# Four graph layers on one core: the second layer's tiles turned by DMA, four banks for its projections, weight low parts moved on VectorE, feature rows padded

## The chip, the core and the metric

The kernel runs on one core of one Trainium2 chip. The metric is the time of one execution on the device in microseconds (us), the lower the better. The engines are TensorE (PE), VectorE (DVE), ScalarE (ACT), GpSimd (POOL) and SyncE (SP); the last issues most DMAs.

## The reference

x is 2048 × 256, adj a sparse 2048 × 2048 matrix of zeros and ones. Four layers follow each other, each `x = layernorm(x + layer(x))`:

```
L0(x) = adj @ (x W0) + b0                                     # W0: 8 heads side by side, 256 x 256
L1(x) = mean over 4 heads of softmax(leaky_relu(src_i + dst_j, 0.01) + adj_ij) @ (x W)
                                                              # src, dst = (x W) . a, two vectors a head
L2(x) = relu(conv(h, W2, b2) + h), h = conv(x, W1, b1)        # conv(f) = relu([f, adj @ f] W + b)
L3(x) = relu(D^-1/2 (adj + I) D^-1/2 x W3)                    # D: row sums of adj + I
```

## The kernel before

Rows are cut into T = 16 tiles of 128. Every factor that goes into a matmul is split into a high and a low float16 part (hi = f16(v), lo = v - hi); a product is hi·hi + hi·lo + lo·hi. adj stays in SBUF as bf16 for the whole kernel; SP loads it in 16 blocks of 1 MB in float32 into four stages, and VectorE (even numbers) and ScalarE (odd numbers) cast them; a cast frees the stage for the load four numbers later.

The program has these stages, counted by k for the preparation of an input and by a for an aggregation (adj @ features):

- `joint(0)`: x is split, turned and projected with W0 (k = 0), and the first four output tiles of the aggregation a = 0 grow beside it (`group0`).
- `rest(0, 1, ...)`: output tiles t = 4 to 15 of a = 0, each 16 steps j of two matmuls (`agg_step`: the stationary block adj[:, j, tile], the high row and then the low row of feature tile j). In layer 0 the high row has a 257th column of ones that gives the row sums. In each tile the preparation of layer 1 (k = 1) is put in between.
- `values_half`: layer 1's values, 256 × 1024, two halves of 512 columns a tile. Among the first of them are the last projections of k = 1 and then TensorE's turning of the source scores (`s_c` at 2T). After this come maximum, biases and shifts on VectorE, and `value_lo`.
- attention: 8 groups (4 heads × 2 column halves) of 16 steps of 24 matmuls.
- k = 2 and a = 1, k = 3 and a = 2, k = 4 and a = 3: the two convolutions and the last layer.

**Preparation of layer 1's tile t (k = 1).** Output tile t of a = 0 ends in PSUM bank t % 4. VectorE adds x (`first`, `s_sum`, which frees the bank for output tile t + 4), takes statistics (`stats`, `aggregate_stats`), GpSimd makes the inverse deviation (`inv_std`, L1107), VectorE normalises (`normalise`, L757) and writes the high part into one of four slots `xs` (`split`, L815), GpSimd writes the low part (`prep_lo`, L1114). TensorE turns the 512 columns by four transposes of 128 × 128 (`transpose`, L499) into PSUM, ScalarE copies them to `xt` (`take_t`, L334), TensorE projects with 8 columns (`project`, L533) and VectorE takes the result into `sd` (`take`, L733). In `rest` the transposes of tile t - 5 stand at j = 4 of output tile t and its projection at j = 10. Projections of k = 1 use banks 6 and 7 in turn, so each waits for the take two tiles back.

**Order on VectorE in layer 0.** `lines` holds the steps of output tiles 0 to 3, `other_sums` those of 4 to 15. In the latter, `one(t)` mixes in turn: first(t), normalise(t-1), stats(t), split(t-1), aggregate_stats(t), take(t-4), and then a step of `fill` if t has one. `fill` (L920) holds work that is due some time: casts of adjacency blocks and low parts of weights (`weight_lo`), and `was_lo`, the low part of the eight columns for `project`. After split(15) come the takes 12 to 15.

**Waits by hand.** `cast_ready` (L625) is called at j = 0 and j = 8 of every output tile and waits for the casts; at t = 5 it also waits for `s_was`, which was_lo gives:

```
                if isinstance(t, int) and t == R + 1:
                    pe.wait_ge(s_was, 1)
```

Layers 2 to 4 turn most of their tiles by DMA from SP's queue already. Feature rows lie in `pset`, one pair of rows of 2 × 258 float16 a tile (1032 bytes); the value rows of the attention in `val`, 258 float16 (516 bytes) each, four heads after each other (L129).

Of the kernel before, what the change touches and what calls it, by code (L numbers as in the profile page):

```python
# [7 lines left out]
def graph_stack(nc, x_in, adj_in, w0_in, b0_in, w1_in, a_in, w2a_in, b1_in, w2b_in, b2_in, w3_in, out):  # L8
# [43 lines left out]
    with ctx:  # L52
# [62 lines left out]
        PSET = T * 2 * PW // 2  # L115
        pset = [part(arena, (s * PSET, (s + 1) * PSET), F16, "p (t q f) -> p t q f", t=T, q=2) for s in range(2)]
# [40 lines left out]
        s_tc = [sem(f"s_tc{i}") for i in range(2)]  # L157
        s_w, s_ph, s_c = sem("s_w"), sem("s_ph"), sem("s_c")
# [55 lines left out]
        EARLY = T - R - 1  # L214

        def by_pe(k, t):

            return k * T + t if k < 2 else 2 * T + (k - 3) * (T - EARLY) + t - EARLY

# [4 lines left out]
        def prep_bank(k, u):  # L224

            return ps[:, 4 + u if k == 2 else 6 + u % 2, :]
# [92 lines left out]
        def _(act):  # L319
# [18 lines left out]
            def take_p(k, t, u):  # L338
                act.wait_ge(s_w, t + (k * T + 1))
                b = prep_bank(k, u)  # L340
                dst = pset[k % 2][:, at(t, 1), 0, 0:D].rearrange("p a f -> p (a f)")
# [22 lines left out]
            def lagged(k, first=0):  # L364

                def one(t, u):
                    take_t(k, t, u)
                    if k != 1:
                        take_p(k, t, u)
                tiles(act, first, T, one)  # L370
# [119 lines left out]
            for k in (3, 4):  # L490
                tiles(act, 0, EARLY - EARLY % R, lambda t, u: take_p(k, t, u))
                for t in range(EARLY - EARLY % R, EARLY):
                    take_p(k, t, t % R)
                lagged(k, EARLY)
# [3 lines left out]
        def _(pe):  # L498
# [11 lines left out]
            def project(k, t, u):  # L510
                if k == 0 and isinstance(t, int) and t == 0:
                    pe.wait_ge(s_wl, 1)
                if k == 2:
# [12 lines left out]
                bank = prep_bank(k, u)  # L526
# [12 lines left out]
                width = w.shape[3]  # L539
                for n, (a, b, kk) in enumerate(steps):  # L540
                    ins = nc.tensor.matmul(bank[:, 0:width], xpart(a, kk), w[:, b, kk, :],  # L541
                                           start=(n == 0), stop=(n == len(steps) - 1))
                ins.then_inc(s_w, 1)

            def agg_step(a, k, it, bank, j, done):
# [4 lines left out]
                nc.tensor.matmul(ps[:, bank, 0:width], lhs, pp[:, j, 0, 0:width], start=(j == 0), stop=False)  # L550
                ins = nc.tensor.matmul(ps[:, bank, 0:D], lhs, pp[:, j, 1, 0:D], start=False, stop=(j == T - 1))  # L551
# [34 lines left out]
            def rest(a, knext, ready):  # L586

                k = (0, 2, 3, 4)[a]

                def one(t, u):  # L590
                    pe.wait_ge(s_sum, t + (a * T - R + 1))
                    prep = knext is not None and not (isinstance(t, int) and t == R)
# [125 lines left out]
        def _(dve):  # L718
# [9 lines left out]
            def take(k, t, u):  # L728

                b = prep_bank(k, u)  # L730
# [6 lines left out]
                hi = pset[k % 2][:, at(t, 1), 0, 0:D].rearrange("p a f -> p (a f)")  # L737
                lo = pset[k % 2][:, at(t, 1), 1, 0:D].rearrange("p a f -> p (a f)")
# [23 lines left out]
            def stages(a, k, t, u):  # L762
# [52 lines left out]
                def split():  # L815

                    if k < 3:
                        dve.wait_ge(s_t, t + (k * T - R + 1))
# [36 lines left out]
            def other_sums(a, k, fill={}):  # L855


                def one(t, u):
# [3 lines left out]
                    if k is not None and not (isinstance(t, int) and t == R and a > 0):  # L862
                        late_.append(lambda: take(k, t - R, u))
# [5 lines left out]
                peeled = max(len(fill), 1)  # L869
# [5 lines left out]
                if k is not None:  # L875
                    for t in range(T - R, T):
# [37 lines left out]
            def was_lo():  # L914
# [12 lines left out]
            for t, (early, late_) in enumerate(lines):  # L927
                for st in early[1:]:
                    st()
                fill[t]()  # L930
# [5 lines left out]
            other_sums(0, 1, {t: fill[t] for t in range(R, 2 * R)})  # L936
# [135 lines left out]
        def _(pool):  # L1072
            nc.gpsimd.memset(ident[:, :], 0.0).then_inc(s_id0, 1)
            nc.gpsimd.memset(pset[0][:, :, 0, D:D + 1], 1.0).then_inc(s_one, 1)
# [110 lines left out]
```

## Time and profile before

| | us |
|---|---|
| median of 3 runs | 706.26 (705.76 to 706.27) |
| the profiled execution, its time | 704.71 |
| the profiled execution, its span | 702.6 |
| TensorE matmuls busy | 686.1 (98% of the span) |
| VectorE busy | 527.8 (75%) |
| ScalarE busy | 393.6 (56%) |
| GpSimd busy | 148.7 (21%) |
| TensorE's granted clock, mean | 0.999 |

The profile has, beside the busy times, groups of instructions by line, the waits of each engine with what ended them, the chain of work that ended last, and the instructions in order of time. Matmuls overlap each other in it (each is shown with about 272 ns), so their rate is read from the distance of starts. Times are counted from the start of the span. "<-" in brackets names what ended an idle time.

### The profile page before, as it was taken

How to read it: one execution, taken by the hardware profiler on the slowest of the kernel's cores; microseconds unless marked ns; L12 is line 12 of the kernel's file. 1: busy time of each engine (PE TensorE's matmuls, PEld its weight loads, DVE VectorE, ACT ScalarE, POOL GpSimd, SP SyncE). 2: the span in 40 equal slices, each digit the busy share in tenths (PEclk: the TensorE clock that was granted, in tenths of full speed). 3: DMA queues.
4: the chain of work that ended last, by engine and by line, in shares of the span. 5: the costliest groups of instructions: out<-in, count | busy, mean ns of one | idle time of the engine just before them, and what ended most of it. 6: DMA issues, size and time to landing. Idle time of an engine off the chain costs nothing.

```text
span 702.6 us, 16657 instructions
## 1 busy us (share of the span) xinstructions
PE 686.1 (98%) x5962; PEld 567.2 (81%) x5962; DVE 527.8 (75%) x985; ACT 393.6 (56%) x525; POOL 148.7 (21%) x239
## 2 busy tenths in 40 slices
PE   6989999999999999999999999999999999999996
PEld 4878854688888888888888888876677778888885
DVE  5888646999898989989899898998432325874564
ACT  7554146888989889798898989643100020223000
POOL 4966422000100000000000000654011102432222
PEclk9999999999999999999999999999999999999999
DMA  8986001000303012030300303013121000210011
GB/s 327 413 311 261 0 3 60 1 1 31 62 31 61 0 42 49 30 60 0 80 10 30 60 0 60 2 29 70 23 46 31 8 1 16 39 30 2 31 49 42
DMA packets 33147, 42.17 MB, mean 60 GB/s; under 512 B 21776, under 2 KB 27856, under 8 KB 30928
## 3 DMA queue, kind: packets, MB, share of 16 engines
q1 hardware_dynamic: 30528, 33.73, 14.7%
q0 software_dynamic: 2016, 7.34, 5.6%
q8 instruction: 28, 0.46, 0.3%
q10 hardware_dynamic: 560, 0.52, 0.2%
q14 instruction: 15, 0.12, 0.1%
HBM read 27.13 MB, written 2.13 MB: 42 GB/s over the span
## 4 chain that ended last, share of the span: by engine, by line
PE 89%; DVE 7%; ACT 1%; issue 1%; DMA 1%; POOL 1%; DVEq 0%; SPq 0%; POOLq 0%; ACTq 0%
PE ps L550 15%; PE ps L551 15%; PE ps L692 14%; PE ps L694 14%; PE ps L693 14%; PE ps L541 9%; PE ps L642 5%; DVE ring_hl L986 2%; DVE ring_a L981 2%; PE ps L504 1%; DMA x<-in_x 1%; DVE x L759 1%; POOL ring_a L1116 0%; DVE stat L753 0%; PE ps L533 0%
## 5 line engine op out<-in xcount | busy, mean ns | idle before, releaser
L694 PE MATMUL ps<-arena,ring_hl 128*128 (+1 forms) x1024 | 279.6, 273 | 0.0
L692 PE MATMUL ps<-arena,ring_hl 128*128 (+1 forms) x1024 | 278.9, 272 | 0.4 <-DVE ring_hl L986 0.4
L693 PE MATMUL ps<-arena,ring_hl 128*128 (+1 forms) x1024 | 278.6, 272 | 0.0
L550 PE MATMUL ps<-arena,adj 128*128 128x256 f16 (+1 forms) x1024 | 230.5, 272 | 0.5 <-issue 0.5
L551 PE MATMUL ps<-arena,adj 128*128 128x256 f16 x1024 | 230.6, 273 | 0.0
L981 DVE SCALAR_TENSOR_TENSOR ring_a<-rho,gam,ring_a 128x1024 f32<-128x1024 f32 x128 | 163.8, 1280 | 18.0 <-ACT ring_a L435 18.0
L986 DVE TENSOR_TENSOR ring_hl<-ring_a,ring_hl 128x1024 f16<-128x1024 f32 x128 | 156.6, 1223 | 6.0 <-ACT ring_hl L449 5.9
L449 ACT ACTIVATE ring_hl<-ring_a 128x1024 f16<-128x1024 f32 x128 | 135.2, 1056 | 44.3 <-PE ps L694 31.0
L435 ACT ACTIVATE ring_a<-adj,shift 128x1024 f32<-128x1024 bf16 x128 | 145.6, 1138 | 0.0
L550 PEld LDWEIGHTS ps<-arena,adj 128*128 (+1 forms) x1024 | 99.9, 98 | 18.2 <-issue 0.7
L551 PEld LDWEIGHTS ps<-arena,adj 128*128 (+1 forms) x1024 | 99.5, 97 | 16.1
L692 PEld LDWEIGHTS ps<-arena,ring_hl 128*128 128x128 f16 x1024 | 100.0, 98 | 12.8 <-DVE ring_hl L986 0.9
L693 PEld LDWEIGHTS ps<-arena,ring_hl 128*128 128x128 f16 x1024 | 99.1, 97 | 13.7
L694 PEld LDWEIGHTS ps<-arena,ring_hl 128*128 128x128 f16 x1024 | 99.5, 97 | 13.1
L1139 POOL DMA_DIRECT2D x<-y x14 | 12.3, 880 | 308.3 <-ACT y L464 308.3
L345 ACT ACTIVATE arena<-ps 128x256 f16<-128x256 f32 (+1 forms) x48 | 18.5, 385 | 96.1 <-PE ps L541 95.8
L741 DVE SCALAR_TENSOR_TENSOR arena<-ps,w 128x256 f32<-128x256 f32 (+1 forms) x32 | 13.5, 422 | 56.1 <-ACT arena L345 56.0
L336 ACT ACTIVATE ring_hl<-ps 128x512 f16<-128x512 f16 (+1 forms) x42 | 25.0, 597 | 42.0 <-PE ps L504 42.0
L1111 POOL TENSOR_TENSOR rstd<-veps,neghalf 128x1 f32<-128x1 f32 x64 | 44.5, 696 | 5.0
L642 PE MATMUL ps<-w,ring_hl 128*128 128x512 f16 x192 | 42.7, 379 | 0.6 <-DVE arena L964 0.6
L1116 POOL TENSOR_TENSOR ring_a<-x,ring_a 128x256 f16<-128x256 f16 (+1 forms) x38 | 31.9, 842 | 43.4 <-DVE ring_a L829 39.9
L759 DVE TENSOR_SCALAR x<-total,mv,rstd 128x256 f32<-128x256 f32 (+1 forms) x48 | 19.8, 411 | 26.3 <-POOL rstd L1111 26.3
(91 smaller groups left out, 553.7 us busy)
## 6 DMA issues: line engine op xcount, KB each, us to landing
arena<-in_adj SPq DMA_DIRECT2D x16, 1024.0 KB, 9.1
x<-y POOLq DMA_DIRECT2D x14, 512.0 KB, 5.2
rho<-s_scratch SPq DMA_DIRECT2D x8, 512.0 KB, 3.7
out_x<-x SPq DMA_DIRECT2D x16, 128.0 KB, 1.7
x<-in_x SPq DMA_DIRECT2D x3, 512.0 KB, 6.9
arena<-in_L_gnn_W SPq DMA_DIRECT2D x1, 1024.0 KB, 16.4
arena<-in_L_gnn_a SPq DMA_DIRECT2D x1, 1024.0 KB, 19.4
rho<-in_L_gnn_W SPq DMA_DIRECT2D x2, 512.0 KB, 10.4
```

Of the source, the lines that this page charges most:

```text
L435: nc.scalar.activation(ring_a[:, jt % SLOTS, :], adj[:, jt, q * CH:(q + 1) * CH], ACT.Exp, bias=shift[:, at(h, 1), jt]).then_inc(s_e, 1)
L449: nc.scalar.activation(ring_hl[:, jt % SLOTS, 0], ring_a[:, jt % SLOTS], ACT.Copy).then_inc(s_ah, 1)
L541: ins = nc.tensor.matmul(bank[:, 0:width], xpart(a, kk), w[:, b, kk, :], start=(n == 0), stop=(n == len(steps) - 1))
L550: nc.tensor.matmul(ps[:, bank, 0:width], lhs, pp[:, j, 0, 0:width], start=(j == 0), stop=False)
L551: ins = nc.tensor.matmul(ps[:, bank, 0:D], lhs, pp[:, j, 1, 0:D], start=False, stop=(j == T - 1))
L642: ins = nc.tensor.matmul(ps[:, 2 * u + half, :], xtt[:, (a * K2 + kk) * P:(a * K2 + kk + 1) * P], w1[:, b, kk, half * 512:(half + 1) * 512 ...
L692: nc.tensor.matmul(acc, hi, v_hi, start=(jt == 0), stop=False)
L693: nc.tensor.matmul(ps[:, b, 0:D], hi, v_lo, start=False, stop=False)
L694: ins = nc.tensor.matmul(acc, lo, v_hi, start=False, stop=(jt == T - 1))
L981: nc.vector.scalar_tensor_tensor(a, rho[:, q, :], gam[:, at(h, 1), jt], a, op0=ALU.max, op1=ALU.mult)\
L986: nc.vector.tensor_sub(ring_hl[:, jt % SLOTS, 1], ring_a[:, jt % SLOTS], ring_hl[:, jt % SLOTS, 0])\
L1111: nc.gpsimd.tensor_tensor(rstd[:, slot:slot + 1], veps[:, slot:slot + 1], neghalf[:, 0:1], ALU.pow)\
```

## The change

Five things are changed:

- Layer 1's 16 tiles are turned by DMA transposes that ScalarE issues, one semaphore for each of the four slots (`s_tg`, `gat_turned`), in place of TensorE's transposes and ScalarE's copies. ScalarE's casts of adjacency blocks 7 and 9 move ahead by one place.
- The projection of tile t - 7 (`TURN_LAG`) instead of t - 5 stands in output tile t, and the takes follow: take(t-7) instead of take(t-4) in VectorE's `one(t)`. Tiles 9 to 15 are projected among the first six value halves: tile 9, tiles 10 and 11, 12, 13, 14 and 15 behind one half each. Projections of tiles 0 to 8 use four banks (4 to 7) and wait for the take four tiles back, those of 9 to 15 use banks 6 and 7 as before.
- VectorE's split waits for the DMA transpose of the tile whose slot it takes.
- On VectorE the low parts of w2a, w2b, w3 and w1 move from output tiles 0, 1, 3 and 5 to 8, 9, 10 and 11 with 12; was_lo moves from tile 0 to tile 1, behind cast 6.
- A pair of feature rows takes 264 + 256 float16 (1040 bytes), so that each row starts at a multiple of 16 bytes. The value rows are not changed.

```diff
-        PSET = T * 2 * PW // 2
-        pset = [part(arena, (s * PSET, (s + 1) * PSET), F16, "p (t q f) -> p t q f", t=T, q=2) for s in range(2)]
+        LOW = D + 8
+        PSET = T * (LOW + D) // 2
+        pset = [part(arena, (s * PSET, (s + 1) * PSET), F16, "p (t f) -> p t f", t=T) for s in range(2)]
...
+        TURN_LAG = R + 3
+        def gat_turned(t, u):
+            return s_tg[u], (t - u) * 4 + 16
-        def prep_bank(k, u):
-            return ps[:, 4 + u if k == 2 else 6 + u % 2, :]
+        def prep_bank(k, t, u):
+            four = k == 2 or (k == 1 and not (isinstance(t, int) and t >= T - TURN_LAG))
+            return ps[:, 4 + u if four else 6 + u % 2, :]
... ScalarE
-            casts_after = {0: 7, 1: 9, 2: 11, 4: 13, 5: 15}
-            for t in range(R + 2):
-                take_t(1, t, t % R)
+            cast_n(7)
+            casts_after = {0: 9, 2: 11, 4: 13, 5: 15}
+            for t in range(T):
+                act.wait_ge(s_lo, T + t + 1)
+                act.dma_start_transpose(xt[:, t, :].rearrange("p (c i) -> p c i", c=2 * K2),
+                                        xs[:, t % R, :, :].rearrange("p q f -> p (q f)")).then_inc(s_tg[t % R], 16)
                 if t in casts_after:
                     cast_n(casts_after[t])
-            lagged(1, R + 2)
... TensorE, project
+                if k == 1:
+                    pe.wait_ge(*gat_turned(t, u))
-                elif k == 2:
+                elif k == 2 or (k == 1 and not (isinstance(t, int) and t >= T - TURN_LAG)):
                     pe.wait_ge(s_c, t + (k * T + 1 - R))
                 elif not (isinstance(t, int) and k == 0 and t < 2):
                     pe.wait_ge(s_c, t + (k * T - 1))
... TensorE, rest
-                        if j == T // 4 and prep and knext < 3:
-                            transpose(knext, t - R - 1, (u - 1) % R)
                         if j == (T - 2 if knext in (3, 4) else T // 2 + 2) and prep:
-                            project(knext, t - R - 1, (u - 1) % R)
+                            project(knext, t - back, (u - back) % R)
... TensorE, the first value halves
-            transpose(1, T - R - 1, R - 1)
-            transpose(1, T - R, 0)
-            for n in range(R):
+            left = list(range(T - TURN_LAG, T))
+            for n, count in enumerate((1, 2, 1, 1)):
                 pe.wait_ge(s_sum, T - R + n + 1)
                 values_half(n // 2, n // 2, n % 2)
-                project(1, T - R - 1 + n, (n - 1) % R)
-                if n < R - 1:
-                    transpose(1, T - R + n + 1, n + 1)
-            pe.wait_ge(s_xt, 2 * T - 1)
-            values_half(2, 2, 0)
-            project(1, T - 1, R - 1)
-            values_half(2, 2, 1)
+                for _ in range(count):
+                    tt = left.pop(0)
+                    project(1, tt, tt % R)
+            for n in range(2):
+                values_half(2, 2, n)
+                project(1, left[n], left[n] % R)
... VectorE, other_sums
-                        late_.append(lambda: take(k, t - R, u))
+                        late_.append(lambda: take(k, t - behind, (u - behind) % R))
...
-                    for t in range(T - R, T):
+                    for t in range(T - behind, T):
                         take(k, t, t % R)
... VectorE, fill
-            fill = {0: was_lo, 1: lambda: weight_lo(3, w2b, w2bf), 2: lambda: cast_n(8),
-                    3: lambda: weight_lo(4, w3, w3f), 4: lambda: cast_n(10), 5: lambda: weight_lo(1, w1, w1ff),
-                    6: lambda: cast_n(12), 7: lambda: cast_n(14)}
+            fill = {1: was_lo, 2: lambda: cast_n(8), 4: lambda: cast_n(10), 6: lambda: cast_n(12),
+                    7: lambda: cast_n(14), 8: lambda: weight_lo(2, w2a, w2af), 9: lambda: weight_lo(3, w2b, w2bf),
+                    10: lambda: weight_lo(4, w3, w3f), 11: lambda: weight_lo(1, w1, w1ff, [0]),
+                    12: lambda: weight_lo(1, w1, w1ff, [1])}
...
                 if t == 0:
                     cast_n(6)
-                    weight_lo(2, w2a, w2af)
```

## Rows read from the trace of the kernel before

**Rows 1.** The page, chain that ended last: shares of the span by engine.

```profile
PE 89%; DVE 7%; ACT 1%; issue 1%; DMA 1%; POOL 1%; DVEq 0%; SPq 0%; POOLq 0%; ACTq 0%
```

**Rows 2.** TensorE in order of time (start, us, engine line), output tile 5.

```profile
43.30 0.27 PE L550 MATMUL ps<-arena,adj 128*128 128x257 f16 x1
...
46.61 0.40 PE L504 MATMUL ps<-ident,ring_a 128*128 128x128 f16 x4 [2.26 <-POOL ring_a L1116]
46.84 0.27 PE L550 MATMUL ps<-arena,adj 128*128 128x257 f16 x1
```

**Rows 3.** VectorE in order of time, tiles 0 and 1 of layer 0.

```profile
42.51 0.18 DVE L916 SCALAR_TENSOR_TENSOR was<-wa,was 128x16 f16<-128x16 f32 x1 [0.51 <-ACT was L397]
...
43.28 0.41 DVE L829 TENSOR_SCALAR ring_a<-total,mv,rstd 128x256 f16<-128x256 f32 x1
43.60 1.22 DVE L722 CAST adj<-arena 128x2048 bf16<-128x2048 f32 x1
44.74 1.29 DVE L910 SCALAR_TENSOR_TENSOR w2a<-rho,w2a 128x512 f16<-128x512 f32 x2
45.95 0.42 DVE L800 BATCH_NORM_STATS2 stat<-total 128x6 f32<-128x256 f32 x1
...
46.50 1.26 DVE L910 SCALAR_TENSOR_TENSOR w2b<-rho,w2b 128x512 f16<-128x512 f32 x2
```

**Rows 4.** VectorE in order of time, tiles 5 to 8: splits (L829), normalisations (L759).

```profile
58.66 0.40 DVE L829 TENSOR_SCALAR ring_a<-total,mv,rstd 128x256 f16<-128x256 f32 x1
...
59.12 2.83 DVE L910 SCALAR_TENSOR_TENSOR w<-arena,w 128x1024 f16<-128x1024 f32 x2
...
62.66 0.41 DVE L759 TENSOR_SCALAR x<-total,mv,rstd 128x256 f32<-128x256 f32 x1 [0.31 <-POOL rstd L1111]
...
63.33 0.39 DVE L829 TENSOR_SCALAR ring_a<-total,mv,rstd 128x256 f16<-128x256 f32 x1
...
66.34 0.41 DVE L759 TENSOR_SCALAR x<-total,mv,rstd 128x256 f32<-128x256 f32 x1 [0.94 <-POOL rstd L1111]
...
70.83 0.40 DVE L829 TENSOR_SCALAR ring_a<-total,mv,rstd 128x256 f16<-128x256 f32 x1
...
72.90 0.41 DVE L759 TENSOR_SCALAR x<-total,mv,rstd 128x256 f32 x1 [0.96 <-POOL rstd L1111]
```

**Rows 5.** DMA issues by line: transposes of layers 2 to 4, median us to landing.

```profile
ring_hl<-ring_a SPq DMA_TRANSPOSE x38, 2.4
```

**Rows 6.** All engines in order of time, end of layer 0's preparation and first values.

```profile
93.79 0.41 DVE L829 TENSOR_SCALAR ring_a<-total,mv,rstd 128x256 f16<-128x256 f32 x1
...
96.63 0.30 PE L533 MATMUL ps<-was,ring_hl 128*128 128x8 f16 x6
...
98.08 0.29 PE L533 MATMUL ps<-was,ring_hl 128*128 128x8 f16 x6
...
103.30 2.98 PE L642 MATMUL ps<-w,ring_hl 128*128 128x512 f16 x13 [0.55 <-DVE arena L964]
```

**Rows 7.** TensorE in order of time: j = 0 of layer 2; a whole output tile.

```profile
476.14 0.27 PE L550 MATMUL ps<-arena,adj 128*128 128x256 f16 x1
...
477.01 1.46 PE L541 MATMUL ps<-w2a,ring_hl 128*128 128x512 f16 x6
478.31 0.27 PE L550 MATMUL ps<-arena,adj 128*128 128x256 f16 x1
...
514.96 0.27 PE L550 MATMUL ps<-arena,adj 128*128 128x256 f16 x1
...
518.50 1.46 PE L541 MATMUL ps<-w2b,ring_hl 128*128 128x512 f16 x6
```

**Rows 8.** VectorE in order of time: fourth reciprocal behind attention groups 0, 1, 2.

```profile
175.41 0.17 DVE L1001 RECIPROCAL rden<-ps 128x1 f32<-128x1 f32 x1 [0.16 <-PE ps L694]
...
217.54 0.17 DVE L1001 RECIPROCAL rden<-ps 128x1 f32<-128x1 f32 x1 [0.16 <-PE ps L694]
...
259.67 0.17 DVE L1001 RECIPROCAL rden<-ps 128x1 f32<-128x1 f32 x1 [0.16 <-PE ps L694]
```

More of the change, by code:

```diff
@@ L157, in graph_stack @@
         s_tc = [sem(f"s_tc{i}") for i in range(2)]
+        s_tg = [sem(f"s_tg{i}") for i in range(R)]
         s_w, s_ph, s_c = sem("s_w"), sem("s_ph"), sem("s_c")
@@ L214, in graph_stack @@
         EARLY = T - R - 1
+        TURN_LAG = R + 3
         def by_pe(k, t):
-            return k * T + t if k < 2 else 2 * T + (k - 3) * (T - EARLY) + t - EARLY
+            return t if k == 0 else T + (k - 3) * (T - EARLY) + t - EARLY
+        def gat_turned(t, u):
+            return s_tg[u], (t - u) * 4 + 16
         def conv_turned(t):
             return s_tc[t % 2], 16 * (t // 2 + 1)
-        def prep_bank(k, u):
-            return ps[:, 4 + u if k == 2 else 6 + u % 2, :]
+        def prep_bank(k, t, u):
+            four = k == 2 or (k == 1 and not (isinstance(t, int) and t >= T - TURN_LAG))
+            return ps[:, 4 + u if four else 6 + u % 2, :]
         def by_dma(k, t):
@@ L339, in take_p @@
                 act.wait_ge(s_w, t + (k * T + 1))
-                b = prep_bank(k, u)
-                dst = pset[k % 2][:, at(t, 1), 0, 0:D].rearrange("p a f -> p (a f)")
+                b = prep_bank(k, t, u)
+                dst = pset[k % 2][:, at(t, 1), 0:D].rearrange("p a f -> p (a f)")
                 src = b[:, D:2 * D] if k in (2, 3) else b[:, 0:D]
@@ L362, in joint, with lagged @@
                         between[t - AHEAD]()
-            def lagged(k, first=0):
+            def lagged(k):
                 def one(t, u):
                     take_t(k, t, u)
-                    if k != 1:
-                        take_p(k, t, u)
-                tiles(act, first, T, one)
+                    take_p(k, t, u)
+                tiles(act, EARLY, T, one)
             def w1_hi(kk):
@@ L493, in _ @@
                     take_p(k, t, t % R)
-                lagged(k, EARLY)
+                lagged(k)
         @block.tensor
@@ L512, in project @@
                     pe.wait_ge(s_wl, 1)
-                if k == 2:
+                if k == 1:
+                    pe.wait_ge(*gat_turned(t, u))
+                elif k == 2:
                     pe.wait_ge(*conv_turned(t))
@@ L525, in project @@
                 xtt = tile_of(xt, t)
-                bank = prep_bank(k, u)
+                bank = prep_bank(k, t, u)
                 def xpart(a, kk):
@@ L549, in agg_step @@
                 lhs = adj[:, j, at(it * P, P)]
-                nc.tensor.matmul(ps[:, bank, 0:width], lhs, pp[:, j, 0, 0:width], start=(j == 0), stop=False)
-                ins = nc.tensor.matmul(ps[:, bank, 0:D], lhs, pp[:, j, 1, 0:D], start=False, stop=(j == T - 1))
+                nc.tensor.matmul(ps[:, bank, 0:width], lhs, pp[:, j, 0:width], start=(j == 0), stop=False)
+                ins = nc.tensor.matmul(ps[:, bank, 0:D], lhs, pp[:, j, LOW:LOW + D], start=False, stop=(j == T - 1))
                 if done:
@@ L588, in rest @@
                 k = (0, 2, 3, 4)[a]
+                back = TURN_LAG if knext == 1 else R + 1
                 def one(t, u):
                     pe.wait_ge(s_sum, t + (a * T - R + 1))
-                    prep = knext is not None and not (isinstance(t, int) and t == R)
+                    prep = knext is not None and not (isinstance(t, int) and t < back)
                     for j in range(T):
@@ L728, in take @@
             def take(k, t, u):
-                b = prep_bank(k, u)
+                b = prep_bank(k, t, u)
                 if k == 1:
@@ L736, in take @@
                 dve.wait_ge(s_ph, t + ((k - (k > 1)) * T + 1))
-                hi = pset[k % 2][:, at(t, 1), 0, 0:D].rearrange("p a f -> p (a f)")
-                lo = pset[k % 2][:, at(t, 1), 1, 0:D].rearrange("p a f -> p (a f)")
+                hi = pset[k % 2][:, at(t, 1), 0:D].rearrange("p a f -> p (a f)")
+                lo = pset[k % 2][:, at(t, 1), LOW:LOW + D].rearrange("p a f -> p (a f)")
                 ot = tile_of(own, t)
@@ L815, in split @@
                 def split():
-                    if k < 3:
-                        dve.wait_ge(s_t, t + (k * T - R + 1))
+                    if k == 1 and isinstance(t, int) and t < R:
+                        dve.wait_ge(s_t, T - R + t + 1)
+                    elif k == 1:
+                        dve.wait_ge(*gat_turned(t - R, u))
                     elif k == 3 and isinstance(t, int) and t < R:
@@ L861, in one @@
                         late_ = []
-                    if k is not None and not (isinstance(t, int) and t == R and a > 0):
-                        late_.append(lambda: take(k, t - R, u))
+                    if k is not None and not (isinstance(t, int) and (t < behind or t == R)):
+                        late_.append(lambda: take(k, t - behind, (u - behind) % R))
                     if isinstance(t, int) and t in fill:
@@ L868, in one @@
                             st()
-                peeled = max(len(fill), 1)
+                behind = TURN_LAG if k == 1 else R
+                peeled = max([t - R + 1 for t in fill] + [1])
                 for t in range(R, R + peeled):
@@ L929, in _ @@
                     st()
-                fill[t]()
+                if t in fill:
+                    fill[t]()
                 for st in late_:
@@ L934, in _ @@
                     cast_n(6)
-                    weight_lo(2, w2a, w2af)
-            other_sums(0, 1, {t: fill[t] for t in range(R, 2 * R)})
+            other_sums(0, 1, {t: step for t, step in fill.items() if t >= R})
             dve.wait_ge(s_c, 2 * T)
@@ L1073, in _ @@
             nc.gpsimd.memset(ident[:, :], 0.0).then_inc(s_id0, 1)
[L1074 removed]
+            nc.gpsimd.memset(pset[0][:, :, D:D + 1], 1.0).then_inc(s_one, 1)
             pool.wait_ge(s_id0, 1)
```

## The prediction, made before the changed kernel was run

> **What bounds the kernel now.** I read the span and the chain that ended last first: 89% of the span is TensorE work [rows 1]. An edit shortens the kernel only if it takes time out of TensorE's own sequence or out of one of its few waits, and only where nothing else then arrives late. The edits lie in the first 103 us (layer 0 and the start of layer 1's values) and, for the padding, in all four layers' aggregations. So I read these next: TensorE's rows at output tile 5 [rows 2], VectorE's rows beside them [rows 3], VectorE's pace through layer 0 [rows 4], the end of layer 0 [rows 6], and the rate of the aggregation matmuls [rows 7, 8]. One profiled execution took 704.71 us, its span is 702.6 us, so 2.1 us lie around it; the median of the three runs is 706.26 us, 1.55 us more. I work out a difference and put it on the median.
>
> **The change part by part**
>
> *1. Transposes of layer 1's input.* TensorE loses 16 groups of four transposes. One group occupies 0.23 us (46.61 to 46.84 [rows 2]), so 16 × 0.23 = 3.7 us of TensorE's sequence go, and ScalarE's copies of them with them. Their place is taken by 16 DMA transposes from ScalarE's queue. A DMA transpose lands 2.4 us after its issue [rows 5]. The projection is moved back to seven tiles behind and a slot of the split ring is needed again four tiles later, 10 us and more, so both are covered even at twice or three times 2.4 us beside the adjacency loads.
>
> *2. The stall at tile 5.* TensorE starts tile 5 at 43.30 and at the first transpose waits 2.26 us for GpSimd's low part of tile 0 [rows 2]. That wait goes. What is late next stands in the code: at tile 5, j = 0, `cast_ready` waits for `s_was`, which was_lo gives. Now was_lo starts at 42.51, before that point. In the new order it comes after normalise(0), split(0), cast 6 (from 43.60) and the statistics of tile 1. The statistics start where the low part of w2a now starts, 44.74, and took 0.55 us to the next instruction (45.95 to 46.50) [rows 3]; was_lo then ends near 44.74 + 0.55 + 0.18 = 45.5 us. TensorE waits there from 43.3 to 45.5, 2.2 us. All later matmuls of the tile are queued behind it. The stall changes its cause and hardly its size.
>
> *3. Who is last at the end of layer 0.* VectorE and GpSimd form a chain: split(t-1) on VectorE, low part and inverse deviation on GpSimd, normalise(t) on VectorE. Without extra work normalise comes 2.07 us after the split (70.83 to 72.90); with a cast behind the split 3.01 us (63.33 to 66.34); with both halves of w1's low part, 2.83 us of work, 4.00 us (58.66 to 62.66) [rows 4]. From a normalise to the split behind it are 0.67 us (62.66 to 63.33 [rows 4]). So a plain tile costs 2.74 us, one with a cast 3.68 us, one with half of w1 0.67 + 2.07 + 1.93/2 = 3.71 us. The low parts of w2a and w2b (1.29 and 1.26 us) are as long as the cast (1.22 us) [rows 3] and I price them as it; w3's, with half their elements, I take at 3.2 us, between plain and cast.
> In the new order the chain runs: normalise(0) 42.95 (0.33 before the split at 43.28 [rows 3]); normalise(1) 43.28 + 3.01 = 46.3; normalise(2), with cast 8, 46.3 + 0.33 + 3.01 = 49.6; normalise(3) 49.6 + 0.33 + 2.07 = 52.0; normalise(4), with cast 10 ahead of its statistics, about 55.9. Then 5 plain 58.6; 6 and 7 with casts 62.3 and 66.0; 8 and 9 with w2a and w2b 69.7 and 73.4; 10 with w3 76.6; 11 and 12 with the halves of w1 80.3 and 84.0; 13 to 15 plain 92.2. Split(15) starts at 92.5; in the kernel before it starts at 93.79 [rows 6]. The total of VectorE's work is the same, only its order differs, so the chain wins 1.3 us, and not the 3.7 us that TensorE is relieved of.
>
> *4. The lag of seven tiles.* In the kernel before, takes 12 to 15 come after split(15) on VectorE, and TensorE needs take 12 only for projection 14. In the new one takes 9 to 15 come after split(15), and project(1, 11) waits for take 9 (`s_c` at t + T - 1). It stands after only the second half of the values. So TensorE gets past projection 11 not before 92.5 + 0.3 (split) + 0.2 (take) = 93.0. Between the starts of projections 11 and 15 lie four value halves and four projections, each pair 1.45 us (96.63 to 98.08 [rows 6]): 93.0 + 4 × 1.45 = 98.8 us for the start of projection 15. Before, it started at 98.08 [rows 6]. From there the chain is the same as now: take 15, maximum, GpSimd's reduction, biases, first low value, next values at 103.30, where TensorE already waits 0.55 us [rows 6]: 5.22 us. So the attention begins at about 104.0 instead of 103.3: **+0.7 us**. The 3.7 us of transposes turn into waits at projections 9, 10 and 11. This term's lower bound: if extra work on VectorE delayed GpSimd only by half of what I priced (4.3 us for the five low parts over the plain pace), -2.1 us, so -1.4 us; its upper bound is rival 2. Behind 103 us nothing of this part is left.
>
> *5. Padding.* 2048 aggregation matmuls read feature rows. Before, a row pair is 1032 bytes, so tile j's high row starts at 0 (j even) or 8 (j odd) bytes past a multiple of 16, the low row at 4 or 12; after, all at 0. A row of output tiles in layers 2 and 3 takes 32 matmuls in 3.54 us (514.96 to 518.50), 110.6 ns each; eight with j = 0 alone, whose high row is aligned, take 0.87 us (476.14 to 477.01), 108.8 ns [rows 7]. With 10 ns of rounding I take 1.3 ns gained in each of the 3 × 12 × 32 = 1152 matmuls of such rows behind the attention, 1.5 us, and 0.5 ns in the other 384, 0.2 us: **-1.7 us**. The 512 of layer 0 gain about as much each, but end in the waits of step 4. Ends of this term: 0 [rows 8], and, at the rate of the 512-column matmuls (six from 477.01 to 478.31 [rows 7], 108.3 ns per 256 columns, 107.5 with the rounding), 3.1 ns × 1152 + 384 × 1.5 ns = -4.2 us. The row against it: attention matmuls read value rows at 4 × head bytes past a multiple of 16. The groups of head 0 (aligned) and of head 1 (not) both take 42.13 us [rows 8]. The Trainium skill (SBUF — State Buffer, Specifications) says SBUF has 16-byte cachelines and that crossing to a new one costs; by that alone head 1 should be slower than head 0, and the trace doesn't show it; by it the sum would still be that of this step.
>
> Sum: +0.7 - 1.7 = -1.0 us, 706.26 - 1.0 = **705.3 us**. Its own range, from the bounds of step 4's lower end and 0 to 4.2 us of padding: 701 to 707.
>
> **The rivals**
>
> *Rival 1: padding does nothing.* For it: head 0 and head 1 [rows 8]. Then only step 4 is left: 706.26 + 0.7 = 707.0 us.
>
> *Rival 2, the other side: the tail is late by more.* VectorE's low parts hold up GpSimd for their whole length instead of part of it. Full length is 1.29 + 1.26 + 1.0 (w3's, an estimate from half of w2b's elements and no less than 0.63) + 2 × 1.41 (half of 2.83 each) = 6.4 us, priced above at 0.94 + 0.94 + 0.46 + 0.97 + 0.97 = 4.3 us, so 2.1 us more in the chain; every microsecond by which split(15) is later goes whole into projection 11. +2.8 us without a gain of padding: 709.1 us; with it 707.4. It decides from the point at which split(15) starts after 93.2. Against it: w1's 2.83 us cost 1.93 us [rows 4]. The Trainium skill (SBUF — State Buffer, SBUF: two separate sides) has VectorE and GpSimd share a port pair as an exclusive lock on which the loser fully blocks; by that rule the low parts would be priced in full where GpSimd has work for all their length.
>
> *Rival 3: TensorE's saving arrives.* If the chain of step 3 keeps pace (a low part costs nothing where GpSimd waits anyway), split(15) falls near 90 us, projection 11 no longer waits, and 2 us are won there: 706.26 + 0.7 - 2.8 - 1.7 = 702.5 us.
>
> *Rival 4: padding gives its far end*, 706.26 + 0.7 - 4.2 = 702.8 us.
>
> **How the numbers follow.** Forecast 40%, rival 1 22%, rival 2 15%, rival 3 15%, rival 4 8%. The range is 702.4 to 708.3: it takes in rivals 1, 3 and 4 and half of rival 2. 0.2% is 1.4 us, about what a measurement of this kernel can tell from no change. Faster by more: rivals 3 and 4, and a third of the forecast's cases (its -1.0 is near the line), 0.36. Slower by more: most of rival 2 and a fifth of rival 1, 0.18. Within: 0.46.
>
> **What would show it.** TensorE stalls about 2.2 us at tile 5's first matmul, put down to VectorE's was_lo; split(15) on VectorE starts near 92.5 us; TensorE waits at projections 9 to 11 for VectorE's sd; the values go on at about 104.0 us; a row of 32 matmuls in layers 2 and 3 takes 3.50 us instead of 3.54. The prediction is wrong if split(15) comes before 91 or after 94 us, if a DMA transpose takes over 10 us beside the loads, or if the row of 32 stays at 3.54 or falls below 3.47.

## The result and the profile after

| | before | after |
|---|---|---|
| median | 705.82 us (704.42 to 706.27) | 714.19 us (707.03 to 722.62) |
| the profiled execution's span | 702.6 us | 710.4 us |
| first attention matmul in it | 134.39 us | 143.45 us |

The changed kernel is slower: ratio 1.0092 with a 95% interval of 1.0064 to 1.0119. The longest of its seven executions, 722.62 us, fell in a slower state of the chip and is left out of the ratio; the other six still spread over 8.6 us (707.03 to 715.66), where those of the kernel before spread over 2. I had forecast 705.3 us and a range up to 708.3.

The chain that ended last, asked for the stretch from 44 to 112 us only, names the cause (start, us, what; this is its longest piece):

```profile
by line: DMA ring_hl<-ring_a 31.6%; PE ps L561 18.8%; PE ps L562 18.3%; PE ps L652 11.1%; PE ps L544 3.2%; POOL rstd L1123 2.5%; issue 2.4%; DVE x L767 2.3%; POOL veps L1121 2.2%; POOL ring_a L1128 2.1%; DVE ring_a L839 1.9%; DVE adj L730 1
...
50.66 21.50 DMA ring_hl<-ring_a
```

One DMA transpose, that of tile 2, takes 21.50 us; in layers 2 to 4 one takes 2.4 us [rows 5]. TensorE's waits after (engine line <- releaser: us, times, longest):

```profile
PE ps L544 <- DMA ring_hl<-ring_a: 8.5, 2, 6.4
PE ps L561 <- DVE was L927: 2.2, 1, 2.2
PE ps L544 <- DVE sd L741: 1.2, 1, 1.2
```

And the instructions in order of time (start, length, engine, line; the wait ahead in brackets): TensorE at output tile 5, ScalarE's issue of two transposes, TensorE's projection of tile 0, VectorE's split of tile 5 (which waits for the slot of tile 1), ScalarE's cast of block 13, VectorE's split of tile 6 (for the slot of tile 2), and the projection of tile 2:

```profile
44.93 0.27 PE L561 MATMUL ps<-arena,adj 128*128 128x257 f16 x1 [2.18 <-DVE was L927]
...
53.19 15.29 ACTq L409 DMA_TRANSPOSE ring_hl<-ring_a  x2
...
56.37 0.30 PE L544 MATMUL ps<-was,ring_hl 128*128 128x8 f16 x6 [2.08 <-DMA ring_hl<-ring_a]
...
61.72 0.41 DVE L839 TENSOR_SCALAR ring_a<-total,mv,rstd 128x256 f16<-128x256 f32 x1 [2.54 <-DMA ring_hl<-ring_a]
...
68.57 1.91 ACT L393 ACTIVATE adj<-arena 128x2048 bf16<-128x2048 f32 x1 [13.50 <-issue]
...
72.19 0.41 DVE L839 TENSOR_SCALAR ring_a<-total,mv,rstd 128x256 f16<-128x256 f32 x1 [6.48 <-DMA ring_hl<-ring_a]
...
72.40 0.56 PE L544 MATMUL ps<-was,ring_hl 128*128 128x8 f16 x6 [6.38 <-DMA ring_hl<-ring_a]
```

The first transpose, issued at 44.73 us, released TensorE at 56.37, 11.6 us later; the second, issued at 47.29, released VectorE at 61.72, after 14.4 us. Issuing those of tiles 3 and 4 held ScalarE's queue for 15.29 us, and ScalarE stood idle for 13.50 us ahead of its cast. Most of that cost nothing: the load of block 13, issued at 48.7 us, landed after 17.2 us, at 65.9, so the cast came 2.6 us late, and no wait of TensorE is put down to it. Of the first row, the wait for was_lo, more below. At the end of layer 0 split(15) stands at

```profile
102.41 0.41 DVE L839 TENSOR_SCALAR ring_a<-total,mv,rstd 128x256 f16<-128x256 f32 x1
```

and not near 92.5 us: one of the signs of being wrong that the prediction named.

What the DMA engines did meanwhile (us, busy time of PE, PEld, DVE, ACT, POOL with counts, granted clock of TensorE, DMA share, GB/s):

```profile
54.00:56.00 2.00, 0.30 (x3) 0.01 (x1) 1.40 (x8) 1.07 (x1) 0.74 (x2) 1.00 0.11 47
...
58.00:60.00 2.00, 2.00 (x11) 1.42 (x10) 0.75 (x2) 0.00 (x0) 0.39 (x1) 0.50 0.51 180
60.00:66.00 6.00, 6.00 (x50) 4.64 (x48) 2.79 (x8) 0.00 (x0) 2.30 (x3) 0.90 1.01 366
66.00:72.00 6.00, 0.03 (x1) 0.00 (x0) 0.00 (x0) 1.91 (x1) 0.00 (x0) 0.95 1.12 265
72.00:78.00 6.00, 5.60 (x30) 4.05 (x31) 4.87 (x15) 1.91 (x1) 3.86 (x5) 0.50 0.29 58
```

In 54 to 56 us loads are under way and the transposes of tiles 0, 1 and 2 are unfinished, and only 47 GB/s move. The last column but two shows a second cost: after TensorE's waits its clock is granted at 0.50, the lower of its two levels (1.2 GHz), in 58 to 60 and in 72 to 78 us. There two matmuls that follow each other start 0.21 us apart, elsewhere 0.11:

```profile
73.09 0.42 PE L562 MATMUL ps<-arena,adj 128*128 128x256 f16 x1
73.30 0.42 PE L561 MATMUL ps<-arena,adj 128*128 128x257 f16 x1
```

The DMA packets of 54 to 58 us, together and by queue (count, MB, share of the 16 engines' time; q1 carries SP's loads, q10 ScalarE's transposes):

```profile
DMA packets 62, 0.25 MB, mean 61 GB/s; under 512 B 33, under 2 KB 33, under 8 KB 33
...
q1 hardware_dynamic: 31, 0.24, 14.2%
q10 hardware_dynamic: 31, 0.01, 0.9%
```

The loads have 31 packets, 29 of 8 KB and two of a few bytes (33 in all are under 512 bytes), and the transposes 31 of 256 bytes: as many of the one as of the other, as if they took turns. 14.2% and 0.9% of 16 engines are 2.4 busy engines, of which the loads' packets have nearly all.

### The profile page after: what moved, and what is told of

It is laid out like the page before. It is cut to its first block, busy times and chain, and to the rows that moved or that the text cites. A ratio compares the mean times of both kernels' runs of the same rounds, so it can differ in the third digit from the quotient of the medians.

```text
span 710.4 us, 16440 instructions
## 1 busy us (share of the span) xinstructions
PE 684.1 (96%) x5898; PEld 566.5 (80%) x5898; DVE 528.6 (74%) x985; ACT 384.5 (54%) x509; POOL 150.4 (21%) x239
## 4 chain that ended last, share of the span: by engine, by line
PE 81%; DVE 7%; DMA 4%; POOL 4%; issue 1%; ACT 0%; SPq 0%; POOLq 0%; DVEq 0%; ACTq 0%
PE ps L700 14%; PE ps L702 14%; PE ps L701 14%; PE ps L561 13%; PE ps L562 13%; PE ps L552 7%; PE ps L652 5%; DMA ring_hl<-ring_a 3%; DVE ring_hl L998 2%; DVE ring_a L993 2%; POOL x L1107 2%; POOL ring_a L1116 1%; DMA total<-in_L_gnn_b 1%; DVE x L767 1%; POOL rstd L1123 0%
## 5 line engine op out<-in xcount | busy, mean ns | idle before, releaser
L561 PEld LDWEIGHTS ps<-arena,adj 128*128 (+1 forms) x1024 | 101.2, 99 | 20.3 <-issue 3.1
L562 PEld LDWEIGHTS ps<-arena,adj 128*128 (+1 forms) x1024 | 101.2, 99 | 15.6
L1123 POOL TENSOR_TENSOR rstd<-veps,neghalf 128x1 f32<-128x1 f32 x64 | 47.4, 740 | 5.0
L1121 POOL TENSOR_TENSOR veps<-mv,epsv 128x1 f32<-128x1 f32 x64 | 16.3, 254 | 99.8 <-DVE mv L812 75.7
```

What stands on the lines that cost most here:

```text
L561: nc.tensor.matmul(ps[:, bank, 0:width], lhs, pp[:, j, 0:width], start=(j == 0), stop=False)
L562: ins = nc.tensor.matmul(ps[:, bank, 0:D], lhs, pp[:, j, LOW:LOW + D], start=False, stop=(j == T - 1))
L1123: nc.gpsimd.tensor_tensor(rstd[:, slot:slot + 1], veps[:, slot:slot + 1], neghalf[:, 0:1], ALU.pow)\
```

## The experiments

I held two theories. A: the DMA transposes of layer 1 run beside the adjacency loads, and one queue's small packets wait behind the other's large ones; all else of the change is about what the prediction says. For the wait itself there are three readings: A1, the two queues take turns packet by packet; A2, a transpose and a load in flight hold each other up whatever their packets; A3, what counts is the bytes in flight. C: the new order and the lag of seven lose by themselves. Padding stands apart (B).

### Padding alone

The kernel before, with rows of 264 + 256 float16:

```diff
-        PSET = T * 2 * PW // 2
...
+        LOW = D + 8
+        PSET = T * (LOW + D) // 2
...
```

> The kernel before with the padded feature rows and nothing else. Theory A (the loss of the changed kernel is the DMA transposes of layer 1 beside the adjacency loads, the padding is a gain by itself): the 32 matmuls of an output tile of layers 2 to 4 take 3.49 to 3.50 us instead of 3.54, and the kernel takes 704.0 to 704.5 us against 705.8, a ratio of 0.998. Rival B (the padding costs or does nothing in the kernel before): 705.8 us or more.

Measured: 703.94 us (703.27 to 705.77), ratio 0.9975 (0.9965 to 0.9985). The padding is a gain of its own, B falls. The changed kernel shows the rate in a whole output tile, for which before stand 514.96 to 518.50 [rows 7]:

```profile
524.05 0.27 PE L561 MATMUL ps<-arena,adj 128*128 128x256 f16 x1
...
527.55 0.81 PE L552 MATMUL ps<-w2b,ring_hl 128*128 128x512 f16 x3
```

32 matmuls take 3.50 us, 109.4 ns each, instead of 3.54. From the first attention matmul to the end the spans are 702.6 - 134.39 = 568.2 us before and 710.4 - 143.45 = 566.9 after: 1.3 us won. The edit changes two things, the start of the rows and the length of a pair (1040 bytes instead of 1032); which of them counts was not tried.

### The loads of the last seven blocks cut to an eighth

```diff
-                sp.dma_start(stage[:, n % STAGES, :], adj_n[n]).then_inc(ld_adj[n % STAGES], 16)
+                width = SW // 8 if n >= 9 else SW
+                sp.dma_start(stage[:, n % STAGES, 0:width], adj_n[n][:, 0:width]).then_inc(ld_adj[n % STAGES], 16)
```

> The changed kernel, but the loads of adjacency blocks 9 to 15 bring only the first eighth of their columns (the rest of those blocks is left out of the computation, what lies in the stage is used in its place). Theory A: the transposes of tiles 0 to 3 land 2.4 to 4 us after issue instead of 11 to 22 us, TensorE's waits for DMA (8.5 us) and the half clock behind them go, and the time is 704 to 706 us, as the prediction had it for covered transposes. Rival C (order and lag lose, not the loads): still over 709 us.

This kernel leaves out seven eighths of each of those blocks and so computes something else; its instructions are the same. Measured: 703.87 us (702.89 to 706.73), ratio 0.9972 (0.9958 to 0.9986). The same program with less beside the transposes is 10 us faster than the changed kernel. Its 16 transposes land in (min/median/max)

```profile
DMA to landing us min/median/max: 2.4/2.5/5.0
```

where the changed kernel has 2.4/2.5/21.5. TensorE's waits are now those that the prediction had put there:

```profile
PE ps L545 <- DVE sd L742: 4.2, 3, 2.0
...
PE ps L562 <- DVE was L928: 2.2, 1, 2.2
```

and in order of time, at projections 9, 10 and 11, with split(15) between:

```profile
87.33 0.29 PE L545 MATMUL ps<-was,ring_hl 128*128 128x8 f16 x6 [1.04 <-DVE sd L742]
...
90.05 0.29 PE L545 MATMUL ps<-was,ring_hl 128*128 128x8 f16 x6 [1.12 <-DVE sd L742]
...
91.74 0.41 DVE L840 TENSOR_SCALAR ring_a<-total,mv,rstd 128x256 f16<-128x256 f32 x1
...
92.37 0.30 PE L545 MATMUL ps<-was,ring_hl 128*128 128x8 f16 x6 [2.02 <-DVE sd L742]
...
99.42 0.30 PE L545 MATMUL ps<-was,ring_hl 128*128 128x8 f16 x6
```

Theory C as the cause of the loss falls with this run. But the row behind the last of these waits shows a cost that the prediction hadn't: the value half there takes 2.5 us instead of 1.3, at the lower clock level (0.50 in 92 to 94 us):

```profile
92.53 2.72 PE L653 MATMUL ps<-w,ring_hl 128*128 128x512 f16 x6
```

```profile
92.00:94.00 2.00, 1.63 (x10) 0.75 (x11) 0.47 (x4) 0.00 (x0) 0.67 (x1) 0.50 0.25 50
```

### Packets of 2 KB and of 1 KB

Each load from block 9 on becomes 4 (or 8) DMAs along the columns, and the waits for a block count them:

```diff
-                sp.dma_start(stage[:, n % STAGES, :], adj_n[n]).then_inc(ld_adj[n % STAGES], 16)
+                cuts = CUTS if n >= FIRST_CUT else 1
+                for c in range(cuts):
+                    part_ = slice(c * SW // cuts, (c + 1) * SW // cuts)
+                    sp.dma_start(stage[:, n % STAGES, part_], adj_n[n][:, part_]).then_inc(ld_adj[n % STAGES], 16)
...
```

> The changed kernel with each load of adjacency blocks 9 to 15 cut in four DMAs along the columns, so that a packet carries 2 KB instead of 8 KB; the same bytes. Theory A1 (packets of the two queues take turns on a DMA engine, so a 256-byte packet of a transpose waits behind one large packet each time): the transposes of tiles 0 to 3 land in 4 to 8 us instead of 11 to 22, the kernel takes 705 to 708 us. Theory A2 (whatever their packets, a transpose and a load in flight together hold each other up): transposes still over 10 us, 710 us or more.

> As the run with 2 KB packets, but eight DMAs a load and packets of 1 KB. Theory A1 (packets of the two queues take turns one for one, so the time of a transpose is its 34 packets per DMA engine times the time of a load packet): transposes of tiles 0 to 3, 8 to 10 us with 2 KB, come down to 4 to 6 us. Theory A3 (what counts is the bytes in flight): they stay at 8 to 10 us.

Measured, with 2 KB: 708.65 us (706.66 to 710.45), ratio 1.0041 (1.0028 to 1.0054); with 1 KB: 710.26 us (708.59 to 712.85), ratio 1.0071 (1.0051 to 1.0091). The transposes issued from 44 to 60 us (with 2 KB, to 62) by the DMA issues of each kernel (x count, median us to landing), first with 8 KB packets, then 2 KB, then 1 KB:

```profile
ring_hl<-ring_a ACTq DMA_TRANSPOSE x5, 14.6
```

```profile
ring_hl<-ring_a ACTq DMA_TRANSPOSE x5, 10.1
```

```profile
ring_hl<-ring_a ACTq DMA_TRANSPOSE x5, 6.3
```

The latency falls with the packet of the other queue, at the same total of bytes. This speaks for A1 in its direction, but the sizes are off: with 2 KB 10.1 us instead of 4 to 8 (A2 had said over 10, and 710 us or more, where 708.65 was measured), with 1 KB 6.3 instead of 4 to 6. Packets in 58 to 60 us with 2 KB:

```profile
q1 hardware_dynamic: 370, 0.67, 87.7%
q10 hardware_dynamic: 371, 0.09, 20.9%
```

again as many of the one as of the other. But a load packet takes 87.7% × 16 × 2 us / 370 = 0.076 us there, and 34 of them are 2.6 us; with the 2.4 us of a transpose alone that is 5 us, and 10.1 were measured. So A1's price doesn't come out with small packets. One reason is in the issues: a transpose is issued before the one ahead of it in the same queue has landed. And with 1 KB not only the packets are smaller: SP takes about 0.43 us to issue each 128 KB, 3.5 us for a block, so less is in flight at a time, and A3 isn't excluded by that run. With 2 KB the issues of a block take 4 × 0.45 = 1.8 us, less than moving it (2.9 us at the 366 GB/s of 60 to 66 us above); the 4.5 us that the transposes gain from 8 KB to 2 KB speak for A1 without this doubt.

The time doesn't follow the latency. With 1 KB packets TensorE waits 0.2 us for a transpose, and the loads are what is late: the casts wait for them, in its waits

```profile
ACT adj L401 <- DMA arena<-in_adj: 25.6, 4, 8.7
DVE adj L738 <- DMA arena<-in_adj: 7.0, 3, 5.7
```

ScalarE issues its transposes in order between its casts, so a late block holds them back all the same. The remedy inside two queues moves the wait from one side to the other.

### The transposes in the queue of the loads

```diff
-            for n in range(STAGES + 2, NL):
+            def turn(t):
+                sp.wait_ge(s_lo, T + t + 1)
+                sp.dma_start_transpose(xt[:, t, :].rearrange("p (c i) -> p c i", c=2 * K2),
+                                       xs[:, t % R, :, :].rearrange("p q f -> p (q f)")).then_inc(s_tg[t % R], 16)
...
+            for n in range(STAGES + 2, 10):
                 load_adj(n)
+            for n in range(10, NL, 2):
+                load_adj(n)
+                load_adj(n + 1)
+                turn(n - 10)
+                turn(n - 9)
+            for t in range(NL - 10, T):
+                turn(t)
... ScalarE
-                act.wait_ge(s_lo, T + t + 1)
-                act.dma_start_transpose(xt[:, t, :].rearrange("p (c i) -> p c i", c=2 * K2),
-                                        xs[:, t % R, :, :].rearrange("p q f -> p (q f)")).then_inc(s_tg[t % R], 16)
```

> The changed kernel with layer 1's transposes issued from SP's queue, between the adjacency loads, and not from ScalarE's: tiles 0 and 1 behind loads 10 and 11, 2 and 3 behind 12 and 13, 4 and 5 behind 14 and 15, then the rest. Theory A1 (two queues taking turns is what stretches a transpose): in one queue a transpose runs in one piece behind the loads ahead of it, it lands 3 to 9 us after issue, ScalarE is free for its casts, and the kernel takes 704 to 708 us. Theory A2 (any transpose together with loads is slow): no better than 710 us.

Measured: 704.67 us (702.34 to 707.01), ratio 0.9991 (0.9976 to 1.0006). All the bytes move, and the loss is gone; against the kernel before it is neither a gain nor a loss that can be told. In 44 to 61 us the five transposes have a median of 8.3 us, most of it behind the two loads ahead of them, and one queue moves 5.41 MB in 17 us, where the two queues of the changed kernel moved 3.07 + 0.27 MB in the 16 us from 44 to 60:

```profile
q1 hardware_dynamic: 2285, 5.41, 99.2%
...
ring_hl<-ring_a SPq DMA_TRANSPOSE x5, 8.3
```

No engine waits for these transposes. The two amounts compare unlike work: in the changed kernel loads wait for casts at other times. And the edit does two things at once, one queue for all transfers and a ScalarE that issues none of them; which of them brings how much was not tried apart.

### The order on VectorE alone

Padding and the new `fill`, with TensorE's transposes and the lag of five (the lines of the padding are left out here):

```diff
-            fill = {0: was_lo, 1: lambda: weight_lo(3, w2b, w2bf), 2: lambda: cast_n(8),
-                    3: lambda: weight_lo(4, w3, w3f), 4: lambda: cast_n(10), 5: lambda: weight_lo(1, w1, w1ff),
-                    6: lambda: cast_n(12), 7: lambda: cast_n(14)}
+            fill = {1: was_lo, 2: lambda: cast_n(8), 4: lambda: cast_n(10), 6: lambda: cast_n(12),
+                    7: lambda: cast_n(14), 8: lambda: weight_lo(2, w2a, w2af), 9: lambda: weight_lo(3, w2b, w2bf),
+                    10: lambda: weight_lo(4, w3, w3f), 11: lambda: weight_lo(1, w1, w1ff, [0]),
+                    12: lambda: weight_lo(1, w1, w1ff, [1])}
```

> The kernel before with the padded rows and the new order of work on VectorE (low parts of w2a, w2b, w3, w1 and was_lo later); transposes on TensorE and the lag of five tiles as before. Theory A (only transposes beside loads lose): no DMA transposes here, so 703 to 705.5 us, with about 2 us of waiting at tile 5 for was_lo or for the low part of tile 0. Rival C (the new order on VectorE loses by itself): over 707 us.

Measured: 702.07 us (701.41 to 704.71), ratio 0.996 (0.9943 to 0.9977), better than I had expected and 1.9 us under padding alone; the two intervals (0.9965 to 0.9985 there) overlap, so the times alone don't show a gain of the order. Split(15), at 93.79 us before [rows 6], is at

```profile
92.52 0.41 DVE L830 TENSOR_SCALAR ring_a<-total,mv,rstd 128x256 f16<-128x256 f32 x1
```

1.3 us earlier, and TensorE still waits 2.2 us for was_lo. So the new order costs nothing, and the profile speaks for a gain of about 1.3 us.

### The takes and was_lo earlier

On the kernel with transposes in SP's queue:

```diff
-                        late_.append(lambda: take(k, t - behind, (u - behind) % R))
+                        late_.insert(0 if k == 1 else len(late_), lambda: take(k, t - behind, (u - behind) % R))
...
+                ahead = 2 if k == 1 else 0
+                for t in range(T - behind, T - behind + ahead):
+                    take(k, t, t % R)
                 for st in stages(a, k, T - 1, R - 1)[1]:
                     st()
                 if k is not None:
-                    for t in range(T - behind, T):
+                    for t in range(T - behind + ahead, T):
```

> The kernel with layer 1's transposes on SP's queue, and VectorE's takes moved: in each output tile take(t-7) comes right behind first(t), and takes 9 and 10 before the last normalise and split. Theory D (step 4 of the prediction: with the lag of seven, TensorE waits at projections 9, 10 and 11 for takes that VectorE has put behind other work; 4.4 us of such waits are in the trace of the kernel without this edit): waits for sd fall under 1.5 us and the kernel takes 701 to 703 us, 2 to 3.5 us less. Rival E (another wait takes their place at once, the last transpose or a bank): within 1 us of 704.7.

Measured: 701.44 us (700.26 to 702.62), ratio 0.9941 (0.9922 to 0.996), 3.2 us less than without the edit; the two intervals are apart. TensorE's waits for sd fell from 4.4 us to 0.5, and another of 1.9 us is new:

```profile
PE ps L661 <- DVE arena L988: 1.9, 1, 1.9
...
PE ps L553 <- DVE sd L750: 0.5, 1, 0.5
```

This doesn't show theory D, for the traces put the gain elsewhere. The two profiles' split(15), with the edit and without:

```profile
90.84 0.41 DVE L848 TENSOR_SCALAR ring_a<-total,mv,rstd 128x256 f16<-128x256 f32 x1
```

```profile
94.29 0.41 DVE L848 TENSOR_SCALAR ring_a<-total,mv,rstd 128x256 f16<-128x256 f32 x1
```

The attention starts at 131.58 and at 135.32 us, 3.7 us apart. Of these, 1.6 us lie ahead of split(0), the first split, (43.32 and 44.96 us), where both do the same; split(0) differs by as much between the kernel before and padding alone (43.28 and 44.73), so it isn't the takes' doing. 1.8 us lie between split(0) and split(15): the edit also changed the order of VectorE's steps within a tile (the statistics are now aggregated ahead of the split), and a plain tile costs 2.48 us instead of 2.72. Only 0.3 us lie between split(15) and the attention, where D's gain would have to show. The projections are done earlier there, but the next step is not, as E had it:

```profile
97.85 0.39 POOL L1147 PARTITION_ALL_REDUCE dmb<-dmx  x1 [5.75 <-issue]
```

VectorE's maximum, which it needs, starts at 95.40 us and takes 0.22. Then was_lo back to tile 0:

```diff
-            fill = {1: was_lo, 2: lambda: cast_n(8), 4: lambda: cast_n(10), 6: lambda: cast_n(12),
+            fill = {0: was_lo, 2: lambda: cast_n(8), 4: lambda: cast_n(10), 6: lambda: cast_n(12),
```

> The run before this, and was_lo back in tile 0, ahead of cast 6. The 2.2 us stall at output tile 5 goes. Theory F (the chain of VectorE and GpSimd, not TensorE, sets the end of layer 0's preparation): TensorE only arrives earlier and waits longer at the end, the time falls by less than 1 us against the run before this. Theory G (TensorE's own work sets it): 2 us less, 699 to 701 us.

Measured: 700.37 us (699.48 to 701.56), ratio 0.9924 (0.9902 to 0.9946). This is 1.1 us under the run before it, between F's bound of 1 and G's 2, and the 700.37 us lie in G's range; the intervals of the two overlap. So the times don't decide between F and G. In the profiles split(15) comes at 90.05 instead of 90.84 us and the attention starts 0.8 us earlier too, which is F's reading. The 2.2 us stall is gone and TensorE waits elsewhere, 0.8 us for sd and 0.8 for the last transpose at L553. It is the fastest kernel of this study, faster than both.

## Why the prediction was wrong

**Step 1 failed, and it made the loss.** It called the DMA transposes "covered even at twice or three times 2.4 us beside the adjacency loads". The 2.4 us came from rows of layers 2 to 4 [rows 5], where no adjacency block is loaded; beside the loads the first three took 11.6, 14.4 and 21.5 us, five to nine times as much. The bound had to come from what a packet waits for. A transpose alone is 544 packets in q10 (74.4 to 77.0 us of the kernel after):

```profile
q10 hardware_dynamic: 544, 0.13, 24.9%
```

so 34 for each of 16 DMA engines. A load packet of 8 KB takes 14.2% × 16 × 4 us / 29 = 0.31 us; 34 turns, each behind one load packet, are 10.6 us, near the 11.6 that the first transpose took. The Trainium skill (DMA: Bandwidth & Descriptors, Queues, rings and completion order) says under Arbitration that a DMA engine takes turns between its queues packet by packet; 31 to 31 and 370 to 371 packets agree with it. That loads beside the transposes cause the wait is shown, by the light loads. That the turns set its length is shown for the first transpose only: the 14.4 to 21.5 us of the later ones, and the 10.1 and 6.3 us beside small packets, are longer than this working gives. I had the means for a rival there and named none; "if a DMA transpose takes over 10 us" stands only in the prediction's last sentence. What followed was a chain I hadn't followed either: VectorE's split waits for the slot, GpSimd and the next transpose wait for the split, and in the end TensorE waits for the transpose. The prediction had counted on 10 us and more from one use of a slot to the next, and from the first transpose's issue to its projection the changed kernel has 9.6 us (44.73 to 54.29); 11.6 is more than that.

**The account of the 9 us.** In the profiled executions the attention begins 143.45 - 134.04 = 9.4 us later than with the light loads. TensorE's two waits for DMA are 8.5 us. The lower clock costs 4.6 us by the distances of starts: 1.7 us from 57.5 to 61.3 us and 2.9 from 72.4 to 78.5. Against this, the waits for sd, 4.2 us with the light loads, shrink to 1.2, and the light loads have a stretch of their own at the lower clock, 1.3 us. 8.5 + 4.6 - 3.0 - 1.3 = 8.8 us; 0.5 us more are lost around the projection of tile 1 (61.60 to 62.35 us). So the lower clock costs about half as much as the waits that it follows. When it falls the rows don't say: it fell after the waits of 2.08 and 6.38 us here and after one of 2.02 us with the light loads, and not after the one of 2.18 us at tile 5, nor after one of 2.03 us in the run with the transposes in SP's queue.

**Step 2 was right.** TensorE waits 2.18 us at the first matmul of tile 5 for was_lo; 2.2 was forecast.

**Step 3 was right where its condition held.** Without the loads' disturbance split(15) starts at 91.74 us (forecast 92.5), and 92.52 with the order alone. Counted from split(0), which these runs and the kernel before have at 42.60, 43.36 and 43.28 us, that is 49.1 and 49.2 us against 50.5: 1.3 to 1.4 us won, where 1.3 was forecast. In the changed kernel itself the step-1 waits put split(15) at 102.41 us.

**Step 4 was right in the wait and wrong in what follows it.** TensorE waits at projections 9, 10 and 11, 4.2 us together, and projection 15 starts at 99.42 us (forecast 98.8); 1.3 us of that are the lower clock, which the step hadn't counted. From there, it said, "the chain is the same as now", 5.22 us. It is not. In the kernel before, GpSimd's reduction starts 1.8 us after VectorE's maximum has ended, for no reason that the profile shows; with the light loads (the second pair), with SP's queue and in the changed kernel it starts at once:

```profile
98.62 0.22 DVE L940 TENSOR_REDUCE dmx<-sd 128x4 f32<-128x64 f32 x1
...
100.66 0.39 POOL L1123 PARTITION_ALL_REDUCE dmb<-dmx  x1 [5.61 <-issue]
```

```profile
99.96 0.22 DVE L953 TENSOR_REDUCE dmx<-sd 128x4 f32<-128x64 f32 x1
...
100.32 0.39 POOL L1136 PARTITION_ALL_REDUCE dmb<-dmx  x1 [7.32 <-DVE dmx L953]
```

So later projections cost little, for they fill a wait that was there. From split(15) to the attention's start pass 134.39 - 93.79 = 40.6 us before, 41.0 both in the changed kernel and with SP's queue: 0.4 us for the lag of seven, where the forecast has 2.0 (0.7 later at the end, 1.3 earlier at split(15)). The reduction stands at least 6.2 us behind the start of GpSimd's last low part in every run; what holds it there is open.

**Step 5 was right.** 3.50 us a row of 32, as forecast; 1.3 us of the forecast's 1.7 in the spans and 1.7 us in the time of padding alone. Of the rivals, 1 (padding does nothing), 2, 3 and 4 (padding's far end) were not what happened, and the side of rival 2 came true by another mechanism. Without step 1's error the time would have come out near the forecast: the changed kernel takes 703.87 us with the light loads and 704.67 with all loads and the transposes in SP's queue, beside 705.61 for the one before, -1.7 and -0.9 where -1.0 was forecast. Part of that nearness is luck: with the light loads the stretch at the lower clock (+1.3 us) and the wait of GpSimd that is gone (-1.7) nearly cancel, and neither was in the sum.

## What to carry to other kernels

Before moving work to a DMA, count its packets per DMA engine and ask what else is in flight in other queues: many small packets in one queue beside few large ones in another can cost a large packet's time each, and more where several such transfers follow each other; and everything that waits for a slot of that ring is late with them. Putting both in one queue, small work at a chosen place between the large transfers, gave back all of the loss here. A wait also costs what the clock loses behind it. And work that is late costs only what the next step isn't waiting for anyway: ask of the step behind it, too, what it waits for. Where an engine issues DMAs between its own work, a slow issue is a wait in front of that work: what is queued behind it belongs in the working.

## What the hardware showed that I had not expected

- Issuing a DMA transpose, 1.2 us alone, held ScalarE's queue for 15.29 us for two of them while the earlier ones were unfinished. Beside packets of 2 KB no issue took over 1.32 us, with transposes of up to 12.2 us; what makes an issue wait is open.
- With two queues in turn the DMA engines moved 47 GB/s in 54 to 56 us with transfers of both kinds pending. In 54 to 58 us the two queues have 31 packets each; why only few engines had work left then is not settled.
- Reading a feature row that starts at a multiple of 16 bytes brought 1.2 ns a matmul in the aggregations (110.6 to 109.4 ns by rows of 32), and no difference between heads in the attention [rows 8]. What makes the two differ was not tried.
